# Transpositions of O's rows and of the maxima moved beside the product with V, in a fused attention and feed-forward kernel

## The reference, cut to what matters

```
qkv = x @ w_qkv.T + b_qkv                     # 16 heads of 16 channels
q, k = rope(elu(q) + 1), rope(elu(k) + 1)
attn = softmax(q @ k.T / 4) @ v               # per head, 1024 x 1024 scores
x = layernorm(x + attn + depthwise_conv3(v))  # "the first norm"
h = relu(k0-signs @ [x, -x]) ; h = relu(k1-signs @ h) ; y = k2-signs @ h
x = layernorm(x + y)                          # "the second norm"
```

## Time and profile before

| what | value |
|---|---|
| median of three runs | 2092.36 us |
| the profiled execution's own time | 2091.6 us |
| its span in the profile | 2089.4 us |
| mean granted TensorE clock | 0.985 |
| TensorE busy | 2031.0 us, 97% |
| VectorE busy | 1684.0 us, 81% |
| ScalarE busy | 1519.8 us, 73% |
| GpSimd busy | 1013.0 us, 48% |

### The profile page before, as it was taken

How to read it: one execution, slowest core, us unless ns; L and a number is a source line. 1 busy time by engine, 2 the same in 40 slices (tenths; PEclk the granted TensorE clock), 3 DMA queues, 4 the chain that set the end, 5 groups by cost and what they waited for, 6 DMA issues and landing times.

```text
span 2089.4 us, 47276 instructions
## 1 busy us (share of the span) xinstructions
PE 2031.0 (97%) x18910; PEld 845.3 (40%) x18910; DVE 1684.0 (81%) x3094; ACT 1519.8 (73%) x2867; POOL 1013.0 (48%) x583
## 2 busy tenths in 40 slices
PE   5999999999999999999999999999999999999998
PEld 3133323444434444344443443444443444444355
DVE  8989988788787988888787887878888788888243
ACT  3399888766877678876787767787687777877742
POOL 2958287614757067462584427752385603400110
PEclk7699999999999999999999999999999999999999
DMA  5001210020010200121000200002001020000000
GB/s 199 20 17 47 72 24 30 17 79 12 17 37 30 82 17 11 35 77 40 11 26 27 86 26 17 29 17 97 14 17 37 19 72 17 13 13 29 2 21 21
DMA packets 40443, 77.10 MB, mean 37 GB/s; under 512 B 15024, under 2 KB 19488, under 8 KB 37280
## 3 DMA queue, kind: packets, MB, share of 16 engines
q1 hardware_dynamic: 34496, 49.97, 8.4%
q0 software_dynamic: 5184, 23.07, 3.0%
q10 hardware_dynamic: 544, 1.05, 0.1%
HBM read 46.27 MB, written 25.17 MB: 34 GB/s over the span
## 4 chain that ended last, share of the span: by engine, by line
PE 82%; DVE 9%; ACT 6%; issue 2%; DMA 0%; SPq 0%; POOL 0%; POOLq 0%; ACTq 0%
PE o_bank L705 21%; PE unit_banks L821 17%; PE unit_banks L661 16%; PE unit_banks L796 8%; PE unit_banks L671 6%; DVE maxima L1100 6%; PE unit_banks L835 5%; PE unit_banks L732 5%; ACT probs L923 4%; PE unit_banks L720 2%; DVE hT L1169 1%; PE unit_banks L713 1%; DMA lepe_rows<-in_b_v 0%; ACT rows L1011 0%; DVE rows L1229 0%
## 5 line engine op out<-in xcount | busy, mean ns | idle before, releaser
L1100 DVE TENSOR_REDUCE maxima<-unit_banks 128x1 f32<-128x512 f32 x2048 | 1312.6, 683 | 258.7 <-PE unit_banks L661 257.3
L923 ACT ACTIVATE probs<-unit_banks 128x512 f32<-128x512 f32 x2048 | 1144.3, 605 | 446.6 <-PE unit_banks L671 423.0
L671 PE MATMUL unit_banks<-q_stack,k_stack 50*128 50x512 f16 x2048 | 698.1, 382 | 10.6 <-ACT probs L923 6.4
L661 PE MATMUL unit_banks<-k_stack,q_stack 48*128 48x512 f16 x2048 | 699.5, 387 | 4.8 <-DVE maxima L1100 3.1
L705 PE MATMUL o_bank<-probs,v_pair 128*32 128x256 f32 x8192 | 565.4, 387 | 4.0 <-issue 4.0
L821 PE MATMUL unit_banks<-h0T,w 64*128 64x512 f16 x3520 | 527.4, 376 | 0.2
L1513 POOL TENSOR_TENSOR attn<-o_rows_sb,rden 128x256 f32<-128x256 f32 x63 | 39.2, 622 | 747.1 <-DVE rden L1113 739.4
L705 PEld LDWEIGHTS o_bank<-probs,v_pair 128*32 128x32 f32 x8192 | 207.0, 109 | 306.4 <-issue 140.2
L661 PEld LDWEIGHTS unit_banks<-k_stack,q_stack 48*128 48x128 f16 x2048 | 153.1, 94 | 404.3 <-issue 199.7
L821 PEld LDWEIGHTS unit_banks<-h0T,w 64*128 64x128 f16 x3520 | 172.4, 95 | 156.0 <-issue 6.5
L671 PEld LDWEIGHTS unit_banks<-q_stack,k_stack 50*128 50x128 f16 x2048 | 156.0, 93 | 79.2 <-ACT probs L923 35.4
(11 more groups left out here) (153 smaller groups left out, 1765.0 us busy)
## 6 DMA issues: line engine op xcount, KB each, us to landing
rows<-in_x POOLq DMA_DIRECT2D x8, 1024.0 KB, 6.4
q_stack<-q_scratch SPq DMA_DIRECT2D x128, 64.0 KB, 2.0
k_stack<-k_scratch SPq DMA_DIRECT2D x128, 64.0 KB, 2.0
work<-in_xT SPq DMA_DIRECT2D x7, 1024.0 KB, 7.5
q_scratch<-parts POOLq DMA_DIRECT2D x14, 512.0 KB, 3.4
k_scratch<-parts POOLq DMA_DIRECT2D x14, 512.0 KB, 3.2
out<-rows SPq DMA_DIRECT2D x7, 1024.0 KB, 5.5
q_stack<-q_scratch SPq DMA_DIRECT2D x128, 32.0 KB, 1.9
```

Of the source, the lines that this page charges most:

```text
L661: nc.tensor.matmul(units.out(unit), q_stack[row:row + STACK, r, t * P:(t + 1) * P], k_stack[row:row + STACK, r, half * 512:(half + 1) * 51 ...
L671: nc.tensor.matmul(units.out(unit), k_stack[row:end, r, kt * P:(kt + 1) * P], q_stack[row:end, r, half * 512:(half + 1) * 512], start=True ...
L923: nc.scalar.activation(probs[:, 2 * (kt % 2) + h, half * 512:(half + 1) * 512], units.out(unit), ACT.Exp, scale=exp_regs[2 * (n % PAIRS) + ...
L1100: nc.vector.reduce_max(maxima[:, v // T % 2, h * T + t, half:half + 1], units.out(unit), AXIS_X)\
```

## The change

In smooth steps alone, the transposition of O's rows or of the maxima no longer stands behind the second score turn. It stands behind the fourth quarter of the L1 piece, directly before the product with V. ScalarE's copy of O's rows follows in such a step behind the second pair of exponentials and no longer before them. VectorE splits the maxima in the step after, behind the first two row maxima of that step; before, it did so behind the first two row maxima of the same step. `program_order`, from which the banks are given, is changed in the same way: the bank of the maxima stays taken from the end of the smooth step to the middle of the next. The first norm is applied in steps 14 to 17 in all elements, where it was 13 to 16.

```diff
-NORMALISE_AT = ({13: 0, 14: 2, 15: 4, 16: 6}, {37 + t: t for t in range(T)})
+NORMALISE_AT = ({14: 0, 15: 2, 16: 4, 17: 6}, {37 + t: t for t in range(T)})
...
-    return len(DEALT[s]) == 1 and in_pair(DEALT[s][0][0])
+    return s >= 0 and len(DEALT[s]) == 1 and in_pair(DEALT[s][0][0])
...  program_order
-                for u in own_units(s):
+                for u in own_units(s - 1) if smooth(s - 1) else ():
+                    if u[0] == "max rows":
+                        yield u, False, False, True
+                for u in () if smooth(s) else own_units(s):
                     yield u, True, True, True
...
+        for u in own_units(s) if smooth(s) else ():
+            yield u, True, True, u[0] == "O rows"
         if s > 0:
             yield PV, False, False, False
...  TensorE
+            def transpose_rows(s):
+                for unit in own_units(s):
+                    if unit[0] == "O rows":
+                        o_rows(unit)
+                    else:
+                        max_rows_T(unit)
...
-                    if i == 1:
-                        for unit in own_units(s):
-                            if unit[0] == "O rows":
-                                o_rows(unit)
-                            else:
-                                max_rows_T(unit)
-                        if not smooth(s):
-                            for unit, part in DEALT[s]:
-                                dense(unit, part)
+                    if i == 1 and not smooth(s):
+                        transpose_rows(s)
+                        for unit, part in DEALT[s]:
+                            dense(unit, part)
...
+                if smooth(s):
+                    transpose_rows(s)
                 if s > 0 and DEALT[s]:
                     weighted_v(s - 1, 0)
                     weighted_v(s - 1, 1)
...  ScalarE
-                if kt == O_ROWS_STEP and n > 0:
+                if kt == O_ROWS_STEP and n > 0 and not smooth(s):
                     copy_o_rows(n - 1)
...
                 for half in range(2):
                     exp_probs(s, 0, half)
+                if kt == O_ROWS_STEP and n > 0 and smooth(s):
+                    copy_o_rows(n - 1)
...  VectorE
-                for unit in own_units(s):
+                for unit in [*(own_units(s - 1) if smooth(s - 1) else ()), *(() if smooth(s) else own_units(s))]:
                     if unit[0] == "max rows":
                         split_max_rows(unit[1])
```

## The result

The changed kernel took 2104.01 us, the median of five runs (2101.69 to 2104.33). The kernel before took 2091.86 us beside it, also the median of five runs (2090.07 to 2093.67). The ratio is 1.0053, with a 95% interval of 1.0043 to 1.0064. The prediction was 2085.2 us, 7.2 us faster. The kernel is 12 us slower, and the time lies outside the range given. The profiled run of the changed kernel took 2104.03 us, with a span of 2101.9 us and a mean granted clock of 0.985, as before.

A forecast was written before the change was run, and what follows sets the result against it. TensorE's instructions were taken to bound each step, except where a PSUM bank comes free late. Savings of 14.4 and 1.2 us less 8.4 us of longer hold gave 7.2 us less, 2085.2 us; own range 2080 to 2090, whole range 2077 to 2094.

The forecast's parts named there:

- The crossing: TensorE between half-row and full-row shapes: 0.09 us each, one of three saved; 2.5 us in 28 smooth maxima steps without wait.
- O's rows: Smooth steps transposing O's rows: 5.9 us saved in 15 steps with a bank wait, 1.8 us in the other 13.
- The maxima's own steps: Smooth steps transposing the maxima: 28 x 0.09 = 2.5 us saved, and 11 with a bank wait, 4.2 us.
- The norm: First norm one step later, elements 2 to 6: step 14's third T tile waits less, 0.25 five times, 1.2 us.
- The held bank: Maxima's bank taken into the next step, leaving six banks: costs 8.4 us together.
- Step 30: Elements 1 to 6: seven banks taken, so the projection waits for the first T tile's exponential; 3.3 us cost.
- Fourteen steps that begin a new L1 pair: Steps 38 and 62 of elements 1 to 6, 30 and 38 of element 7: 0.1 us each, 1.4 us cost.
- Steps 6 and 7 and 14 and 15: Elements 2 to 7, VectorE and ScalarE already trailing: the split's extra work costs 3.7 us.
- the first rival: Score tiles behind the late bank in all 33 steps after a finished pair: 2094.6 us, no change; chance 0.2.
- The third rival: New bank map also frees the 0.44 us waits in 27 steps that begin a pair: 2073 us; chance 0.1.
- the second rival: DMAs of the maxima land late and TensorE waits, at 3.0 us landing 28 us: 2113 us; chance 0.08.
- The fourth: Rival that the crossing isn't what is paid, so only the waits go: 2092 us; chance 0.05.

The follow-up runs named there:

- the last run: Changed kernel, maxima split first in the next step, T tile estimate 0.6, VectorE unit 0.5, projection's reading put at 1.6 (was 0.65): 2069.75 us.
- O's rows alone: Kernel before with only the transposition of O's rows moved in smooth steps, maxima and norm in their old places: -6.7 us by steps.
- the maxima alone: Kernel before with only the maxima's transposition moved in smooth steps, O's rows and norm in their old places: 25.4 us more.
- the new numbers: Bank-dealing estimates in `Units`: T tile read after 0.6 (was 0.48), VectorE unit 0.5 (was 0.65); changed kernel with them 2081.51 us.
- the runs with other estimates: Kernels with T tile read after 0.6 (was 0.48), VectorE unit 0.5 (was 0.65); kernel before 2083.1 us, changed kernel 2081.51 us.
- TENSOR_SCALAR: Kernel before plus two spare 16x128 TENSOR_SCALARs on VectorE in each step behind smooth maxima, no bank held: 2176.3 us.
- the kernel before with the new estimates: Kernel before, no instruction moved, bank estimates T tile 0.6 (was 0.48) and VectorE unit 0.5 (was 0.65): 2083.1 us.
- the hold alone: Kernel before with only VectorE's split of the maxima moved to the next step, transposition in its old place, own semaphores: 2122.79 us.
- TENSOR_REDUCE: Kernel before plus two spare 16x128 TENSOR_REDUCEs on VectorE in each step behind smooth maxima, no bank held: 2098.36 us.
- the split first with the new numbers: Changed kernel, VectorE splitting the maxima first in the next step, with bank estimates T tile 0.6 and VectorE unit 0.5: 2068.8 us.

## Why the prediction was wrong

**What bounds the kernel: right.** TensorE's distances set a step, and only late banks lengthen one. Plain smooth steps stay at 3.71 us.

**The crossing: right.** Forecast 0.09 us for each, measured 0.10 in 27 steps with the maxima that had no wait (3.92 us against 3.93 forecast) and in O's step 2. The drain of 128 cycles that the Trainium skill, "TensorE: Matmul & The Clock Gate", Step-by-step, gives would be 0.053 us, an estimate. As the price of a crossing it is too small beside the measured 0.10 us, and the rows were the better guide.

**O's rows: nearly right.** Forecast 7.7 us, measured 6.7. Steps 26 and 58, with a wait, gained 0.37 (0.39 forecast), the other steps 0.05 to 0.10 (0.14), the steps behind pay nothing, and ScalarE's later copy cost nothing.

**The maxima's own steps: wrong in eleven.** "So I take the wait as gone: 11 x 0.38 = 4.2 us" failed. The place was read at the exponentials, which read a bank within 1.1 us. But the new map gave these transpositions a bank that a projection held, and ScalarE's activation of it (0.78 us) ended at 865.53. They lost 11 x 0.17 = 1.9 us where 4.2 was to come. The price was right: where another map took the wait away, in step 13 of the last run, the step fell by 0.39.

**The norm: right sign, too small.** Forecast 1.2 us, measured 6.5. The wait of 0.80 us in step 14 went nearly whole in five elements, and the prediction took 0.25 of it on the ground that VectorE would be late next. It was not. The move brought the third T tile of step 14 from 2.29 to 1.14 us into the step. Element 1 gave another 1.6 us by steps 14 to 19. Of these about 1.2 us are a stretch at half clock in steps 15 and 16 that the kernel before had in its profile: the runs with O's rows alone and with the maxima alone lack it too, with the norm in its old place.

**The held bank: the step that failed.** The forecast was 8.4 us, and the maxima alone measured 24.5. The prediction had named "if many steps behind the maxima grow by 0.4 or more" as a sign of being wrong, and 31 of the 39 did. By its terms:

- Step 30: 6 x 0.55 forecast, 6 x 0.64 measured. The count of banks was right. The projection's releaser is a VectorE maximum, not the exponential, since it was given the bank of the step's first S tile.
- "Fourteen steps that begin a new L1 pair ... Between 0 and the 0.44 us I take 0.1, as there is a plain step behind to recover: 1.4 us." They cost 0.88 each, 12.3 us. The price of one wait, 0.44, was right, but the step takes it twice more, so the upper end of the range was too low. That holds for the old numbers of `Units`; with the new ones the hold costs these steps 0.27 to 0.46. And nothing is recovered in a plain step behind: TensorE bounds it, and it lasts 3.71 us whatever came before.
- Step 46 was not in the sum for banks, and cost 3.4 us. Steps 6 and 7 and 14 and 15 were taken at 3.7 us by VectorE's load. By the maxima alone steps 6, 7 and 14 cost 4.4 us, and the 3.5 of step 6 come through banks. Steps 6 and 46 could have been counted as step 30 was: the finished pair's two banks, four score tiles and the maxima make seven, and the projection or unit of V is the eighth. Unlike step 30 they can be served, as the new numbers show, when this unit takes a bank of the finished pair.

This is the first rival, "the held bank eats the gain", which had 0.2. Its mechanism is the one found, and the estimates of `Units` made about half of the price. It put its 33 steps at 14.5 us and so came to no change; the maxima alone cost 20.7 us in these 33. The third rival, better banks for tiles that wait now, did not come by itself, but the runs with other estimates show that it was there to be had: 9 us without any other change. The DMAs of the maxima did not come late in any number that counts. The idle time that they end, for line 580, was 3.2 us in 7 places over the whole run (before, 1.1 in 2):

```profile
  PEld unit_banks L666: 3.2, 7
  PE unit_banks L666: 0.2, 1
```

Those are weight loads, and the steps that start a pair of heads two steps behind those that grew are as long as before, so the second rival is out. The fourth is out with the crossing.

Open: whether any choice of banks can free step 30 and the last 0.27 to 0.46 us of steps 38 and 62 while the bank is held. No run tried another set of numbers for it.

## What to carry to other kernels

Where banks are handed out ahead of time by an estimate, a moved unit changes the whole map; work out the new map and read which score tile stands behind which, before any price is put on the move. A unit that moves towards the end of a step must be read there, too: it is the time from writing to reading that costs, and not the place. And a step that the matrix engine bounds recovers nothing for the one before it, so a wait costs its whole length as often as it stands in the chain. Last, two variants must be compared under the same estimates: the hold cost 27.1 us with one pair of numbers and 12.8 with the other.

## What was not expected of the hardware

**A small VectorE instruction beside GpSimd.** TENSOR_SCALAR on 16x128 values from SBUF to SBUF took 202 ns at best and up to 2399 ns. Of the 78, 38 took 202 to 216 ns, and all but one of these ran while GpSimd had no instruction running. The 39 that took 780 ns or more each started while a GpSimd TENSOR_TENSOR of 2.1 to 2.4 us was running, as the rows at 789.85 and 790.80 show, and each ended within 0.09 us behind the end of that instruction. So the small instruction waited for GpSimd's to end; it was not merely slowed. TENSOR_REDUCE of the same input took 260 to 276 ns in all 78 cases, and the changed kernel's own split, which reads PSUM, 0.27 us. In the step of these rows TensorE then stood still for 3.26 us, until a late row maximum, and behind it ran at half clock, as a windows table of that run shows (busy us of PE, PEld, DVE, ACT, POOL; then the granted clock, DMA share, GB/s):

```profile
791.00:794.70 3.70, 0.49 (x6) 0.10 (x2) 3.67 (x5) 0.70 (x2) 3.62 (x2) 0.93 0.29 65
794.70:801.00 6.30, 6.25 (x38) 2.39 (x38) 3.79 (x7) 3.11 (x6) 5.57 (x3) 0.50 0.01 3
```

So 78 instructions of this kind made 83 us. The Trainium skill, "GPSIMD Engine Reference", section 8, Key points, says that GpSimd shares its SBUF interfaces with VectorE and that VectorE's instructions in a 2-port perf mode contend there. The trace agrees for the instructions that took 0.8 to 2.4 us. Of the same notes, the Trainium skill, "VectorE: DVE Perf Modes", The perf-mode tier table, gives a TENSOR_SCALAR of this type from SBUF twice the base rate, the mode that takes both SBUF read ports, and a TENSOR_REDUCE only the base rate; the 202 ns of the one where GpSimd was idle and the 269 ns of the other agree.

**Half a clock in step 15.** In single elements of the norm's neighbourhood TensorE's granted clock falls to about 0.5, the lower of its two levels (1.2 GHz), for some 3.5 us, behind step 14 with its waits. Windows of the kernel before with the new estimates:

```profile
798.00:800.10 2.10, 2.10 (x18) 0.97 (x17) 2.10 (x6) 2.10 (x6) 2.02 (x2) 0.96 0.34 97
800.10:803.60 3.50, 3.50 (x19) 2.34 (x21) 1.57 (x5) 1.52 (x4) 3.33 (x3) 0.54 0.11 29
```

It costs 1.5 to 1.65 us where it strikes in elements 2 to 6, and 1.2 in element 1, where it reaches into step 16. It struck in other elements in other kernels (element 1 in the kernel before, 3 in the same with the new estimates, 5 with O's rows alone, 2 and 5 with the maxima alone, 1 and 2 with the hold alone, 1, 4 and 6 with TENSOR_REDUCE, 2 to 6 with TENSOR_SCALAR), so about 1.65 us for each strike in any difference between two single profiles may be this. All seven kernels with the norm in its old place have it in their profile, and none of the seven with the norm one step later has it in step 15. One of those, the split first with the new numbers, has such a stretch in steps 17 and 18 of element 1. So a part of what the norm's move is worth is this stretch; how large a part over many runs, no run shows.
